# Eight layers in one kernel on one core: another list of spare products for TensorE

## The chip, the cores and the metric

The kernel runs as one program on one core of a Trainium2 chip. The metric is device time in microseconds (us). The engines are TensorE (PE, with its weight loads shown apart as PEld), VectorE (DVE), ScalarE (ACT), GpSimd (POOL) and SyncE (SP), which only issues DMAs. TensorE runs at one of two clocks, 1.2 or 2.4 GHz; the profile gives the granted one as a share, 0.5 or 1.0.

## The reference

A tensor x of 2048 tokens by 128 channels passes eight layers, each added to x and fed with a layer norm of it:

```
x = x + L0_attn_a(norm(x))   # delta rule: a recurrence over all 2048 tokens, 16 heads of 8x8 state
x = x + L0_ffn(norm(x))      # shared expert and 8 routed ones, top 2
x = x + L0_attn_b(norm(x))   # top 15 of causal logits, gather, small MLP, palette lookup
x = x + L0_ffn(norm(x))
x = x + L1_attn_a(norm(x))   # linear attention, running sums over tokens
x = x + L1_ffn(norm(x))      # sigmoid gate, 8 experts, top 2, relu squared
x = x + L1_attn_b(norm(x))   # decayed state, a recurrence over tokens
x = x + L1_ffn(norm(x))
```

The first one is what can't be spread over tokens:

```
v_old = einsum('bhd,bhde->bhe', k_t, state)
delta = clip(v_t - v_old, -1, 1)
state = state + clip(0.9 * k_t[..., :, None] * delta[..., None, :], -1, 1)
o = clip(einsum('bhij,bhj->bhi', state, q_t), -1, 1)
```

## The kernel before

The 2048 tokens are 16 tiles of 128. Each layer is one or more stages, each a Python generator over the tiles, written once for each engine (front, gram, scan and out for the first layer, pal and mix for the third, lin and dec for the two attentions of L1, ffn0 used twice a tile as ffn2 and ffn4, ffn1 used twice as ffn6 and ffn8, and prep once). A yield cuts a stage into pieces. Tiles of different layers are in work at the same time.

For each engine a long string, ORDER, gives the order of the pieces, one letter for each: z prep, f front, g gram, s scan, o out, a ffn2, p pal, m mix, b ffn4, l lin, c ffn6, d dec, e ffn8. PE's string has 2250 letters. fast() (line 501) walks it: for place n it calls before(n) and then runs the next piece of that letter. Each engine works its instructions strictly in this order; between engines there are only semaphores. The first layer's recurrence (stage scan) runs on DVE (L1033 multiplies, L1041 scans, 1024 steps), and PE gives it two sets of small products for every four steps: four of L610 (32x32, they need DVE's transpose L1013) and four of L621 (they need DVE's mask L1049; DVE reads them at L1056, later in its own order).

A float32 product counts as two in the profile, a bfloat16 product or a transpose as one.

Spare products are PE work whose result nobody reads: 128x128 weights of ones, 512 columns, bfloat16, line 541. How many stand at a place of the order is one digit of the string FILL (lines 200 to 221, 2250 digits). For PE before(n) is fill(n), and the digit is used in bank(), which hands a piece its PSUM bank:

```
533        def bank(key, *until):
535            b, old = bk.take(key, *until)
536            held.extend(old)
537            if idle[0]:
538                free()
539                w.wait_ge(*PV.at("b1", 0))
540            for _ in range(idle[0]):
541                e.matmul(b[:, 0:512], onesb[:, :], ..., start=True, stop=True)
542            idle[0] = 0
543            return b
550        def fill(n):
551            idle[0] = int(FILL[n])
```

So they are written into the bank that the piece then uses, after the wait for that bank and before the piece's other waits. Not every piece takes a bank. In scan the pieces with L610 write into psS, a tile of their own, and at both ends of the recurrence there are empty pieces; in mix the three loops with L764, L788 and L797 write into pb; prep's L950 does too; out's and lin's carry products (L643, L834) and the later pieces of the loops L708, L810 and L929 go on in a bank that an earlier piece took.

Other lines that the steps below name: norm() on PE (L564, a transpose; POOL's L1738 makes what it reads, ACT's L1369 reads its result), front's products (L573, L576; read by ACT L1378, and down that chain DVE L993), gram's (L596, read by ACT L1434), ffn1's up-products (L871, three groups of four; ACT reads each with L1658 and squares it with L1662) and down-products (L880 and L881, two groups, the first of which waits for the second square and the second for the third; read by ACT L1670).

Of the kernel before, what the change touches and what calls it, by code (L numbers as in the profile page):

```python
# [92 lines left out]
def pieces(stage):  # L93
# [104 lines left out]
        "ppppmpppmpppmppmpppmppppmppppmppmppppmpmpppppmpmpppmppepemeppppmpeepemeeeeeeeeee",  # L198
}
FILL = (  # L200
    "091909062040000000025030020020010000010010000100100000010000500001020020000070000901000001020000000000000020"
    "200002000200000000000000000010010001000000100500002000000000000000200000000000000000000000000000400000000001"
    "000000000010000000000110030000000000010000000000100000000020000000000000000000000000000520000000030000000300"
    "000000000000002000020000000010000000000000000000101000000000000000000000000000010000000000000200000000030000"
    "000000000000000002020000000000000200000000000300020000000000010000000000000000000001300000000000000000000000"
    "000000000000000000000000001003001010000000000100300000006000100000000000000000000000000000000000000000000000"
    "000000000000000020000000000000000000000000000100000000000002000000000000003220000000030103000000100300200000"
    "000000000000000000000000000000000000000000000002200000000000000000000000000000000000000000000010000000000010"
    "000000000000003000000000000000000000000000000000000000004030000000000000000000001000000000000000000000000000"
    "000000004000000000000000000000500000000000000000012000000000003000000000100000000000000000100000000000000000"  # L210
    "400000000000000000000000000000000000000000200000000000000000000000000020000520000000006030000000000002000000"
    "000000000000000000000000000000000000000000000000000000000000000000000400000000200000000000000330090006000000"
    "000000000000000000000000000000005000000000000000000000000000000000000000000000000000000000000000000003000000"
    "040000000000000020020003000213000080000000000000000000000000000000000000000000000000000000000000000010000000"
    "000000000002000000001000000000001040000000000001000000000000301000300000005000000000000000000000000100000000"
    "000000000000000000000000000000000000000000000000000000000000000100000000000000000041000000060000000000000050"
    "000000000100000010000000000000200000000000000200040000000000000000000000000000000000000000000000005000000000"
    "820930000000000000020100000000000000000000000000004000100000000000000000200000000000000000000400000000020000"
    "009300472001000000000000000000000000000000000000000000200000000000000000000000000000000000000000062540000100"
    "010000901000010200000000000000100000000000000000000000000000100000000000020000000300000000000000000000000000"  # L220
    "000000001200023000700160100000000001020000000000920005000000920930000200004200000920000920")

# [1951 lines left out]
```

## Time and profile before

| | us |
|---|---|
| median of 3 runs | 1384.04 |
| lowest and highest | 1383.59, 1386.72 |
| the profiled execution | 1393.87 |
| its span, first to last instruction | 1392.1 |
| PE, DVE, POOL, ACT busy in it | 1243.0, 1000.2, 910.7, 820.1 |
| mean granted clock | 0.929 |

The span is all of the profiled execution but 1.8 us; this execution was 9.8 us above the median, so a difference is worked out in its times and then added to the median. Busy time of PE is the union of its products' recorded times, and a recorded product ends some 0.17 us after its last column went in, so short waits of PE are not seen as idle time. In a row of a view an instruction stands with its line in the kernel, and the releaser in brackets is what ended the idle time before it.

### The profile page before, as it was taken

The page shows a single profiled execution, that of the slowest core. Times are in us where ns is not written, and L with a number is a line of the kernel's source. Part 1 is how long each engine was busy: PE and PEld are TensorE (multiplying, and loading weights), DVE is VectorE, ACT ScalarE, POOL GpSimd, SP SyncE. Part 2 cuts the span into 40 slices and gives each one's busy share as a digit, 9 for nine tenths or more (in the row PEclk, how much of TensorE's full clock was granted, in tenths as well). Part 3 has the DMA queues.
Part 4 walks back from the last instruction along what each step waited for, and adds up shares of the span by engine and source line. Part 5 has one row for each costly group of instructions (what it writes and reads, how often), then busy time and mean ns, then how long its engine had stood idle before and what let it go on. Part 6 is the DMA issues. An engine that isn't in the chain of part 4 may idle for free. (4 is left out here: it accounts for less than half of the span.)

```text
span 1392.1 us, 47171 instructions
## 1 busy us (share of the span) xinstructions
PE 1243.0 (89%) x18561; PEld 813.5 (58%) x18561; DVE 1000.2 (72%) x4437; ACT 820.1 (59%) x2193; POOL 910.7 (65%) x1321
## 2 busy tenths in 40 slices
PE   7777797989999998998899999999999999998896
PEld 3333454656566575756656665755666565757654
DVE  3768878778777868787786888978888775464432
ACT  2232253556676576757476666657574657667764
POOL 5353668686968677685776676776857466674541
PEclk8687678989999999999999999999999999999998
DMA  6000101001000000000010000100001010101000
GB/s 175 2 1 5 30 12 31 24 15 28 12 20 19 16 21 11 24 15 19 14 27 12 15 24 8 29 8 23 15 6 32 6 39 10 34 15 31 4 3 7
DMA packets 27257, 29.35 MB, mean 21 GB/s; under 512 B 12146, under 2 KB 22291, under 8 KB 27027
## 3 DMA queue, kind: packets, MB, share of 16 engines
q0 software_dynamic: 8336, 16.73, 4.9%
q1 hardware_dynamic: 18690, 9.51, 2.5%
q8 instruction: 149, 2.44, 0.8%
q14 instruction: 82, 0.66, 0.2%
HBM read 24.90 MB, written 2.29 MB: 20 GB/s over the span
## 5 line engine op out<-in xcount | busy, mean ns | idle before, releaser
L1873 POOL DMA_INDIRECT sb<-table,sb x240 | 241.8, 1007 | 81.5 <-issue 51.1
L1041 DVE TENSOR_TENSOR_SCAN ps<-ps,sb 128x47 f32<-128x47 f32 (+3 forms) x1024 | 271.0, 265 | 30.5 <-ACT sb L1445 1.5
L1033 DVE TENSOR_TENSOR ps<-sb,ps 128x24 f32<-128x24 f32 (+3 forms) x1024 | 193.1, 189 | 14.7
L541 PE MATMUL ps<-sb 128*128 128x512 bf16 x585 | 177.6, 413 | 8.7 <-ACT sb L1658 2.7
L1733 POOL TENSOR_TENSOR sb<-sb 128x1 f32<-128x1 f32 x128 | 73.2, 574 | 138.3 <-DVE sb L976 137.6
L610 PEld LDWEIGHTS ps<-sb 32*32 32x32 f32 x2032 | 41.0, 108 | 107.6 <-DVE sb L1013 65.6
L610 PE MATMUL ps<-sb 32*32 32x32 f32 x2032 | 69.8, 209 | 36.2 <-DVE sb L1013 35.6
L621 PEld LDWEIGHTS ps<-sb 32*32 32x32 f32 x2032 | 41.5, 108 | 93.1 <-DVE sb L1049 54.3
L982 DVE TENSOR_TENSOR sb<-ps,sb 128x128 f32<-128x128 f32 x112 | 32.2, 289 | 80.5 <-PE ps L708 29.8
L541 PEld LDWEIGHTS ps<-sb 128*128 128x128 bf16 x585 | 54.7, 105 | 58.8 <-issue 14.5
L1369 ACT ACTIVATE sb<-ps 128x128 f32<-128x128 f32 x128 | 34.9, 275 | 90.7 <-PE ps L564 90.2
L621 PE MATMUL ps<-sb 32*32 32x12 f32 x2032 | 64.7, 189 | 19.0 <-DVE sb L1049 10.0
L1056 DVE TENSOR_TENSOR ps<-sb,ps 128x12 f32<-128x12 f32 x254 | 40.9, 161 | 51.7 <-PE ps L621 50.3
L708 PE MATMUL ps<-sb 128*128 128x128 f32 x512 | 77.3, 298 | 0.0
L1670 ACT ACTIVATE sb<-ps,sb 128x128 bf16<-128x128 f32 x256 | 70.8, 375 | 8.2 <-PE ps L881 8.0
L596 PE MATMUL ps<-sb 128*128 128x480 f32 x128 | 73.8, 665 | 1.4 <-DVE ps L1056 0.5
L1049 DVE TENSOR_TENSOR sb<-ps,sb 128x32 f32<-128x32 f32 x254 | 45.9, 181 | 39.2 <-PE ps L610 38.1
L1885 POOL TENSOR_TENSOR sb<-sb 128x512 f32<-128x512 f32 (+1 forms) x32 | 47.3, 1485 | 36.0 <-DVE sb L1239 35.8
L764 PE MATMUL ps<-sb 128*16 128x16 f32 x4096 | 64.6, 211 | 6.3 <-issue 4.2
L708 PEld LDWEIGHTS ps<-sb 128*128 128x128 f32 x512 | 68.9, 209 | 1.9 <-issue 1.1
L1772 POOL TENSOR_TENSOR sb<-sb 128x480 f32<-128x480 f32 x64 | 66.0, 1034 | 4.9 <-ACT sb L1408 4.3
L764 PEld LDWEIGHTS ps<-sb 128*16 128x16 f32 x4096 | 54.3, 133 | 24.8 <-issue 18.4
(313 smaller groups left out, 3532.3 us busy)
## 6 DMA issues: line engine op xcount, KB each, us to landing
sb<-table,sb POOLq DMA_INDIRECT x240
sb<-in_cs SPq DMA_DIRECT2D x16, 128.0 KB
table<-sb SPq DMA_DIRECT2D x17, 64.0 KB, 1.5
sb<-dscr SPq DMA_DIRECT2D x64, 2.0 KB
out<-sb SPq DMA_DIRECT2D x16, 64.0 KB, 1.6
sb<-in_x SPq DMA_DIRECT2D x3, 256.0 KB, 5.4
sb<-in_wex SPq DMA_DIRECT2D x1, 512.0 KB, 4.1
sb<-in_rvx SPq DMA_DIRECT2D x1, 512.0 KB, 4.5
```

The costliest lines, as they stand in the source:

```text
L541: e.matmul(b[:, 0:512], onesb[:, :], onesb[:, :].unsqueeze(1).to_broadcast([128, 4, 128]), start=True, stop=True)
L596: e.matmul(b[:, 0:32 * LW], blk, g_.pp[j % 2][:, :], start=True, stop=True).then_inc(*g_.P("s"))
L610: x = e.matmul(psS[rows, 0:32], KZT[c % 2][rows, 32 * o1:32 * o1 + 32], R[g % 2][rows, :], start=g == 0, stop=True, skip_group_check=True)
L621: x = e.matmul(b[rows, 0:12], SB[g % 2][rows, :], KM[c2 % 2][rows, 4 * o2:4 * o2 + 4, :].rearrange("p a b -> p (a b)"), start=True, stop=True)
L708: x = e.matmul(b[:, 0:128], s.hw[j // 4][:, 128 * (j % 4):128 * (j % 4) + 128], wex[:, 128 * j:128 * j + 128], start=False, stop=j == 7)
L764: x = e.matmul(pb[32 * q:32 * q + 16, 16 * k:16 * k + 16], PTt[:, at, :], PTt[:, at, :], start=True, stop=True)
L1033: e.tensor_tensor(at(psP, p + ROW - 3 - 2 * m, [ROW, 3], [2, m], [1, 2]), AC[:, row(n, k), :, HIST - 2 * m:HIST].rearrange("p r (a b) -> p ...
L1041: e.tensor_tensor_scan(at(psD, 16 + k + COMB * skip, [COMB, 3 * ROW - skip]), at(psP, p + skip, [1, 3 * ROW - skip]), Q[:, i % 32, skip:3 ...
L1670: x = e.activation(s.w[:, 128 * at:128 * at + 128], bk.of[s.name, "d", g, c][:, 128 * j:128 * j + 128], ACT.Copy, scale=t[:, 40 + at:41 + at])
L1733: e.tensor_tensor(st[:, 11:12], st[:, 10:11], mhalf[:, 0:1], ALU.pow).then_inc(*s.G("lr"))
L1772: e.tensor_tensor(g_.pp[j % 2][:, :].rearrange("p (a b c) -> p a b c", b=2, c=LW), at(KT[c % 3], 32 * j, [2, 16], [0, 2], [1, LW]), km[:, ...
L1873: e.indirect_dma_start(GA[:, k, :], None, table[0:128 * i + 128, :] if i else table0, bass.IndirectOffsetOnAxis(u[:, k:k + 1], 0)).then_in ...
```

## The change

Only the string FILL differs. The order of the pieces, all stages and all other engines are the same. The old string has 204 digits that aren't zero, with the sum 585; the new one 506, with the sum 1619. Its first three lines of 21, and the last:

```diff
 FILL = (
-    "091909062040000000025030020020010000010010000100100000010000500001020020000070000901000001020000000000000020"
-    "200002000200000000000000000010010001000000100500002000000000000000200000000000000000000000000000400000000001"
-    "000000000010000000000110030000000000010000000000100000000020000000000000000000000000000520000000030000000300"
...
-    "000000001200023000700160100000000001020000000000920005000000920930000200004200000920000920")
+    "001949080000100100025330020120913090215310000000100000010020500001020002103075009901200000220020003000000020"
+    "200062010200000000000004210303010051400000000500502310930000000000200300000000000390000400000000400400002000"
+    "300260000100000020502110330002013000211000000003100803002020030000201000001050800200000520002200010030000000"
...
+    "000000000000002000010260000000100000000200013000922004000108010920000002000319014820009400")
```

## Rows read from the trace of the kernel before

**Rows 1.** The page: busy us of each engine, its share of the span, instructions.

```profile
PE 1243.0 (89%) x18561; PEld 813.5 (58%) x18561; DVE 1000.2 (72%) x4437; ACT 820.1 (59%) x2193; POOL 910.7 (65%) x1321
```

**Rows 2.** Windows: length, busy us of PE, PEld, DVE, ACT, POOL, granted clock, DMA.

```profile
0.00:300.00 300.00, 240.28 (x3067) 133.87 (x3068) 218.07 (x1132) 110.42 (x309) 178.98 (x308) 0.78 0.13 34
300.00:1140.00 840.00, 779.40 (x12459) 524.60 (x12458) 667.32 (x2985) 544.29 (x1447) 600.82 (x854) 0.97 0.07 18
1140.00:1392.10 252.10, 223.31 (x3038) 155.03 (x3036) 114.83 (x323) 165.36 (x438) 130.93 (x160) 0.98 0.06 15
```

**Rows 3.** The same windows for L541 alone; its durations in ns (min/median/max).

```profile
0.00:300.00 300.00, 53.21 (x146) 14.69 (x146) 0.78 0.13 34
300.00:1140.00 840.00, 77.63 (x264) 23.44 (x264) 0.97 0.07 18
1140.00:1392.10 252.10, 46.76 (x175) 16.54 (x175) 0.98 0.06 15
...
L541 PE MATMUL ps<-sb x585: 379/379/634, 1.1 to 1379.7; 128*128 128x512 bf16 x195
```

**Rows 4.** Instructions in order of time near the end: start, length in us.

```profile
1375.60 0.83 PE L871 MATMUL ps<-sb 128*128 128x128 bf16 x12
1376.27 2.11 PE L541 MATMUL ps<-sb 128*128 128x512 bf16 x9
1378.98 0.23 PE L880 MATMUL ps<-sb 128*128 128x128 bf16 x1 [0.60 <-ACT sb L1662]
...
1378.83 0.58 ACT L1658 ACTIVATE sb<-ps 128x512 bf16<-128x512 f32 x1
...
1379.98 0.35 ACT L1670 ACTIVATE sb<-ps,sb 128x128 bf16<-128x128 f32 x1
```

**Rows 5.** The chain of waits of the page, shares of the span by engine.

```profile
POOL 5%; PE 4%; issue 3%; ACT 1%; DVE 0%; DMA 0%; POOLq 0%; DVEq 0%
```

**Rows 6.** The page's group of L610: busy us, mean ns, idle before, releaser.

```profile
L610 PE MATMUL ps<-sb 32*32 32x32 f32 x2032 | 69.8, 209 | 36.2 <-DVE sb L1013 35.6
```

**Rows 7.** The scan's L621 near 592 us and its reader on DVE.

```profile
592.43 0.25 PE L621 MATMUL ps<-sb 32*32 32x12 f32 x8
...
596.40 0.17 DVE L1056 TENSOR_TENSOR ps<-sb,ps 128x12 f32<-128x12 f32 x1
```

**Rows 8.** The same near 1035 us: PE, DVE, ACT.

```profile
1035.28 0.25 PE L621 MATMUL ps<-sb 32*32 32x12 f32 x8
1035.46 1.07 PE L596 MATMUL ps<-sb 128*128 128x480 f32 x2
...
1037.66 0.27 PE L564 MATMUL ps<-sb 128*128 128x128 f32 x1
...
1037.95 0.15 DVE L1056 TENSOR_TENSOR ps<-sb,ps 128x12 f32<-128x12 f32 x1
...
1037.97 0.28 ACT L1369 ACTIVATE sb<-ps 128x128 f32<-128x128 f32 x1 [0.78 <-PE ps L564]
```

**Rows 9.** The start: PE's first products, and what two of them wait for.

```profile
1.12 4.02 PE L541 MATMUL ps<-sb 128*128 128x512 bf16 x9 [1.12 <-DVE sb L1315]
...
3.96 0.81 POOL L1738 TENSOR_SCALAR sb<-sb 128x128 f32<-128x128 f32 x1
...
6.66 0.88 PE L573 MATMUL ps<-sb 128*128 128x384 f32 x2 [0.88 <-DMA sb<-in_cst]
...
14.47 0.35 DVE L993 RECIPROCAL sb<-sb 128x32 f32<-128x32 f32 x1 [2.55 <-DMA sb<-in_bcm]
```

**Rows 10.** The scan's L1041 on DVE in four stretches at either clock.

```profile
142.40:166.30 23.90, 7.73 (x29) 0.50 0.13 35
183.40:200.50 17.10, 5.60 (x21) 1.00 0.04 10
200.50:220.90 20.40, 5.08 (x19) 0.50 0.10 25
220.90:268.70 47.80, 15.96 (x60) 1.00 0.10 25
```

More of the change, by code:

```diff
@@ L200 @@
 FILL = (
-    "091909062040000000025030020020010000010010000100100000010000500001020020000070000901000001020000000000000020"
-    "200002000200000000000000000010010001000000100500002000000000000000200000000000000000000000000000400000000001"
-    "000000000010000000000110030000000000010000000000100000000020000000000000000000000000000520000000030000000300"
-    "000000000000002000020000000010000000000000000000101000000000000000000000000000010000000000000200000000030000"
-    "000000000000000002020000000000000200000000000300020000000000010000000000000000000001300000000000000000000000"
@@ L206 @@
[L206 to L220, printed above, removed]
@@ L221 @@
-    "000000001200023000700160100000000001020000000000920005000000920930000200004200000920000920")
+    "001949080000100100025330020120913090215310000000100000010020500001020002103075009901200000220020003000000020"
+    "200062010200000000000004210303010051400000000500502310930000000000200300000000000390000400000000400400002000"
+    "300260000100000020502110330002013000211000000003100803002020030000201000001050800200000520002200010030000000"
+    "002000040070000000023003249310000003000300014002001000000003700000000400002020003300000000000100200032033000"
@@ new lines @@
+    "000000200000000002020000002001000000000002040309022000000100028003100000000000000001008000000000000000000000"
+    "000000000000000020000001103100535001100000010100330040006000000000000000000000000000000000500000000000005130"
+    "800000000000200020000000000000000000000300003100750000100002005022000000003220100000001201400000040330200030"
+    "200312430000000020050203900000000200100000001045000003000000000300000000000200000000000000000000000000000013"
+    "000000004000103000000000000000000300002079010000320010090000030000220000000000000000200000000000000000000000"
@@ new lines @@
+    "000000000000000000000000000000501001000000080009012000000000000000000000100000000000020602000000020000050000"
+    "400003004000440200010000000000000001000000300020000000000000000000000000000000000325021030310030020003000000"
+    "002400000000500010000000000020020023000020000220000900001000010000000604200600000000000000000400090006000020"
+    "500002000600040000001000000410302011406000000003000020000000000000000000046000002000000000000002000009000000"
+    "040100006000001023020020350003000061020000000000000000000000003000000003000000000000050000000000000020000040"
@@ new lines @@
+    "090000000000000000000000006910000000003100001000000580000000401000300000006534321550000000000000300000000000"
+    "001000000003000031000033000000300003000000001000004010100000000100001000140140000040200009000000000700100000"
+    "071001002000001000000002300210000030130010103000130000402003004000000000000003000000020200050000215300020700"
+    "005960000003500363000000000000000000000000000300003000000000100309080201000000090000000000000000000000000000"
+    "049000850000000000000004020240200003001000000330000200000000000000000020000000000000000000003600063004000000"
@@ L226, in program @@
+    "400200902000000000000042046204010200000004300000020006060000200022000000000003002405600000200010000201222000"
+    "000000000000002000010260000000100000000200013000922004000108010920000002000319014820009400")
 def program(nc, t):
```

## Prediction

> **What bounds the kernel now.** I read the table of engines first [rows 1]. TensorE (PE) is busy 1243.0 of 1392.1 us, DVE 1000.2, POOL 910.7, ACT 820.1. The reader is to see that PE, which runs every layer's pieces in one written order, has only 149.1 us of recorded idleness. Then three windows, for the clock [rows 2]: in the first 300 us the granted clock is 0.78, so PE spent (1 - 0.78) x 2 x 300 = 132 us at 1.2 GHz; from 300 to 1140 us it is 0.97 (some 50 us), after that 0.98 (some 10 us).
>
> Then the spare products themselves, line 541 [rows 3]. There are 585 of them, 146, 264 and 175 in the same three windows. Nine in a row take 2.11 us and the median one alone 0.38, so the next starts (2.11 - 0.38) / 8 = 0.216 us after the one before [rows 3, 4]: that is what one costs PE at 2.4 GHz, and about twice that at 1.2 GHz. All 585 are 126 us. In the trace they mostly stand directly ahead of a wait, as the nine of 1376.27, after which PE still waits 0.60 us for ACT L1662 [rows 4]: they lie in time in which PE had nothing to do, and cost nothing.
>
> Last, who holds the end. The chain of waits, which the profile can follow back only through the last 13% of the span, gives PE 4% and POOL 5% [rows 5]. So PE is about 4/13 = 0.3 of the path where the path is seen. PE itself waits longest ahead of the scan's products L610, 36.2 us, for DVE's transpose L1013 [rows 6].
>
> **What the change really executes.** The diff gives another string FILL and nothing else. fill(n) (line 550) puts the digit of place n into idle[0], overwriting what is there; only bank() (line 533) spends it. A place of the order whose piece doesn't call bank() drops its digit. I walked ORDER["PE"] through the stage functions: 1400 of the 2250 places call bank(). All 204 places of the old string are among them, and its sum, 585, is the count of L541 in the trace [rows 3]. Of the 506 places of the new one 299, with 1011 of the 1619 spare products, are among the 850 that don't call it: 130 in mix (its loops into pb), 100 in scan (the L610 pieces and the empty ones at both ends) and 69 elsewhere. So 608 products at 207 places are executed. Of the 585, 365 stay where they are; 220 go and 243 come, net +23.
>
> **Part 1, the net number.** 23 x 0.216 = +5.0 us of PE time, the upper end, if nothing hides it; the lower end is 0, PE having 149.1 us of idleness to put it in [rows 1]. I take +0.5: near 0, because almost all of the 585 stand in such idleness, as [rows 4] shows.
>
> **Part 2, the 220 that move.** The question is whether their new place is still free. Setting the trace's products against the order, 60 of some 95 places that lose products still have a wait behind them (144 products, 31 us): removing them only lengthens that wait. The others give back at most 76 x 0.216 = 16 us. Of the 243 that come (52 us), only some 7 us fall on a wait at the very same place. That looks bad, but the new place is mostly one or two pieces ahead of the old one, and what counts is when the piece behind is read. Four examples, two of them among the thirteen places that gain five or more (85 products in all), and the start:
> - Place 2246, near the end: 0 to 9 ahead of the third up-product group of the last FFN, and 9 to 4 at the next place, 2 to 0 after it. Its four L871 begin at 1376.05 (twelve from 1375.60, 0.056 each); with 1.94 us ahead, at 1377.99, done by 1378.4. ACT reads them at 1378.83 [rows 4]. The next group (L880, 1378.98) would start at 1378.22 + 4 x 0.216 = 1379.08, 0.1 us late, and ACT L1670 takes it at 1379.98. Cost 0.
> - Place 919: 0 to 9 ahead of L621 of 592.43, whose result DVE L1056 reads at 596.40 [rows 7]; with 1.94 us it is done by 594.7. The next two places lose 7. Cost 0.
> - Place 1709: 0 to 9 ahead of L621 of 1035.28, and 6 to 0 two places on. L1056 reads at 1037.95, in time. But the L596 of 1035.46 behind it moves to 1037.40 and would keep PE until 1038.3, while L564 ran at 1037.66 and ACT had already waited for it [rows 8]. Cost 0.6 us, if ACT L1369 is on the path.
> - Place 1, the first of all: 9 to 0. In the trace these nine run at 1.2 GHz from 1.12 to about 4.9 us, and L564 behind them could not start before POOL L1738 ended at 4.77 [rows 9]. Without them PE is idle at first, and the clock may rise later. Then the L573 and L576 from 6.66 to 8.2 us would take up to 1.3 us more; but DVE L993, two steps down that chain, waits for a DMA until 14.47 [rows 9]. Cost 0, at most 1.3.
> So a moved product costs between 0 and its 0.216 us, and most cost 0. Where none of it were hidden the thirteen big places alone would be 85 x 0.216 = 18 us; the lower bound is the gain of 16 us above, which I don't expect either, as what PE gains ahead of a wait it gives back in the wait. With a path share of 0.3 for the example's kind of miss, at a quarter of the thirteen, 13 x 0.25 x 0.6 x 0.3 = +0.6 us. Nothing is queued differently on DVE, ACT, POOL or SP: no wait and no DMA is changed.
>
> **Part 3, the clock.** Spare products only pay if they keep the clock at 2.4 GHz where it now falls. In the first 300 us the executed number goes from 146 to 127 (nine of the nineteen are place 1's), so I expect no gain there. Later single short stretches remain, 60 us in all by the windows. What one is worth: between 142 and 269 us the trace has two long stretches at 0.50 and two at 1.00 [rows 10]. The scan makes 29 + 19 = 48 steps in 44.3 us at 1.2 GHz (1.08 per us), 21 + 60 = 81 in 64.9 us at 2.4 GHz (1.25 per us). So a microsecond at 1.2 GHz loses 0.13 us of progress, the pace being set by DVE as much as by PE. If 10 us flip either way that is 1.3 us; taken 0.
>
> The Trainium skill prices this otherwise: TensorE: Matmul & The Clock Gate, in its table of terms, gives the penalty as throttled time x (1 - K/N), which at 1.2 GHz is 0.5 us for each microsecond. By that rule the 10 us would be 5 us and not 1.3, and the sum could be 1380 or 1390 in place of 1385. The scan's pace in this trace bears out only a quarter of it. The Trainium skill, TensorE: Matmul & The Clock Gate, Back-to-back issue gap, gives some 131 ns for a product of 512 columns in a sustained stream, by which the net 23 would be 3 us; nine in a row in this trace show 216 ns, and the measurement decides.
>
> **The sum.** Against the profiled execution: span 1392.1, total 1393.9 us, 9.8 us above the median 1384.0 of the runs shown; I take differences and add them to the median. 0.5 + 0.6 + 0 = +1, 1384.0 + 1 = 1385 us. What the measurement can tell from no change is about 0.2%, 2.8 us.
>
> **The rivals.**
> - A, no net change (above): 1385. For it: the executed count moves by 4%, 365 of 585 stay, and moved ones keep readers that come later [rows 4, 7].
> - B, slower: PE delays reach the path. The mechanism is place 1709's, spare products ahead of a piece whose reader follows at once. PE is in order and 89% busy, so a delay of 2 us is not made up for several pieces. If half of the 85 products at the thirteen big places pass through it is 9 us, 1393. It decides from 2.8 us on, which is 13 products, one in seven of the 85. For it: only 7 of 52 us fall on a wait at the same place; against it: 31 us of products vanish from in front of waits right behind.
> - C, faster: the added products lie where the clock fell. Were a third of the late 60 us to go back to 2.4 GHz, it is 20 x 0.13 = 2.6 us by the scan's pace and 10 at most if PE alone set it; with some of the 16 us of part 2 given back, 1384 - 6 = 1378. Against it: the first 300 us, where two thirds of the loss is, get fewer.
> - D, all 1619 are executed. 1034 x 0.216 = 223 us, more than the 149 us of idleness: even with all of it filled +74 us, 1458; if in return all of the 192 us at 1.2 GHz [rows 2] ran at twice the speed, 96 us less, 1362. The middle is 1410. The page would show L541 x1619. By the code this can't be.
>
> **How the numbers follow.** A 0.41, B 0.32, C 0.25, D and anything else 0.02. Faster by over 0.2% is C with half of the rest, 0.26; within 0.2% is A, 0.41; slower is B with the other half, 0.33. Predicted 1385, A's own range 1381 to 1388. The range of 8 in 10 reaches C's 1378 and B's 1393 with a little beyond, as the path before the last 13% isn't seen: 1376 to 1394.
>
> **What would show it.** L541 x608 in the page, some 127 of them before 300 us. PE busy up by about 5 us or less. The granted clock 0.92 to 0.94. Before DVE L1056 no new waits near 592 and 1035 us; under B the 0.78 us that ACT L1369 waits for L564 [rows 8] are over 1 us. PE's wait for ACT L1662 near the end [rows 4] is shorter than 0.3 us in any case. The prediction is wrong if L541 isn't 608, if the clock of the first 300 us leaves 0.78 by more than 0.05, or if the scan ends more than 3 us from where it did, which would say that delays of PE add up in it.

## The result: 0.9% slower, at the same clock

The changed kernel takes 1401.12 us (median of 9 runs, 1396.22 to 1405.42), the kernel before on the same chip 1386.72 (9 runs, 1383.17 to 1394.96): a ratio of 1.0092 with a 95% interval of 1.0072 to 1.0113. That is 13 us more by the ratio (the medians differ by 14), outside the range of 1376 to 1394. The page of the changed kernel, its busy times and its chain of waits by engine (of before: [rows 1, 5]):

```profile
PE 1230.2 (88%) x18584; PEld 814.4 (58%) x18584; DVE 1000.2 (72%) x4437; ACT 821.4 (59%) x2193; POOL 910.1 (65%) x1321
...
PE 40%; POOL 17%; issue 10%; DVE 9%; ACT 6%; DMA 0%; POOLq 0%; DVEq 0%; ACTq 0%
```

The windows of after (length, busy us of PE, PEld, DVE, ACT, POOL, granted clock, DMA), first of all instructions, then of L541 alone (of before: [rows 2, 3]):

```profile
0.00:300.00 300.00, 235.61 (x3070) 131.74 (x3071) 221.83 (x1147) 113.29 (x313) 181.39 (x311) 0.79 0.13 34
300.00:1140.00 840.00, 773.79 (x12471) 525.41 (x12469) 661.67 (x2960) 542.61 (x1442) 596.73 (x850) 0.98 0.07 18
1140.00:1394.40 254.40, 220.81 (x3053) 157.28 (x3049) 116.66 (x332) 165.47 (x439) 132.03 (x162) 0.99 0.06 15
...
0.00:300.00 300.00, 46.92 (x127) 12.85 (x127) 0.79 0.13 34
300.00:1140.00 840.00, 87.97 (x307) 27.39 (x307) 0.98 0.07 18
1140.00:1394.40 254.40, 45.47 (x174) 15.69 (x174) 0.99 0.06 15
```

The reader is to see three things. L541 stands 127 + 307 + 174 = 608 times, so the 299 digits at places without bank() are not executed. The clock isn't lower in any window. And the chain, here followed through 82% of the span, is 40% PE: half of what is seen, where I had taken 0.3 from the visible 13% of before. The chain of e4_tail, which has before's list up to place 1885, is followed through 81% and is 38% PE: so before's own share was nearer to a half too.

One caution on the pair of traces. The profiled execution of after took 1396.22 us, the shortest of its nine and with 0.938 the one of the highest clock (0.928 to 0.938); that of before 1393.9, near the longest of its own. So the two traces differ by 2.3 us only, not by the 13 to 14 us of the runs, and no stage can be read off by laying them side by side. Two kinds of difference lie in them: what the list does, and how long the clock happened to be low. The second can be taken out. Call 2 x (1 - granted clock) x time the "low time" (us at 1.2 GHz). Within the runs of the unchanged kernel before, on four chips (98 runs in five groups), the time rises by 0.29 to 0.34 us for each us of low time. I use 0.3. That range was seen within some 35 us of low time to either side of a mean; where a list moves it further, the last column rests on the price holding there too, which no run shows. The table does this for every kernel that ran, against the mean of before on the same chip (one of f_min's twelve runs, in a slower state, is left out):

| kernel | L541 | ratio [95%] | mean us | low time | left at 0.3 |
|---|---|---|---|---|---|
| e1_dropped | 608 | 1.0089 [1.0055, 1.0124] | +11.4 | -2.8 | +12.2 |
| e2_start | 566 | 1.0024 [0.9995, 1.0053] | +2.9 | +2.0 | +2.3 |
| e3_middle | 628 | 1.0054 [1.0028, 1.0080] | +7.8 | -2.5 | +8.6 |
| e4_tail | 584 | 1.0018 [0.9994, 1.0041] | +1.4 | -0.8 | +1.6 |
| g_tight | 779 | 1.0095 [1.0057, 1.0134] | +14.6 | -13.8 | +18.8 |
| g_slack | 778 | 1.0102 [1.0063, 1.0142] | +15.7 | -7.2 | +17.9 |
| f_min | 365 | 1.0077 [1.0044, 1.0111] | +13.1 | +47.8 | -1.2 |
| f_none | 0 | 1.0316 [1.0269, 1.0364] | +49.4 | +293.7 | -38.7 |
| k_local | 593 | 1.0019 [0.9990, 1.0047] | +3.2 | +3.0 | +2.3 |
| g_slack2 | 778 | 1.0077 [1.0054, 1.0101] | +10.9 | -7.6 | +13.2 |
| g_tight2 | 779 | 1.0155 [1.0124, 1.0186] | +22.9 | +14.6 | +18.5 |
| f_max | 828 | 1.0135 [1.0092, 1.0178] | +17.3 | -4.6 | +18.7 |
| s_swap | 608 | 1.0110 [1.0061, 1.0159] | +14.3 | +26.4 | +6.4 |
| f_min2 | 365 | 1.0147 [1.0104, 1.0189] | +19.9 | +64.3 | +0.6 |
| m_cut | 363 | 1.0109 [1.0068, 1.0150] | +14.6 | +93.9 | -13.6 |
| v_move | 582 | 1.0170 [1.0133, 1.0208] | +23.8 | +61.5 | +5.3 |
| v_late | 582 | 1.0146 [1.0116, 1.0176] | +19.5 | +55.1 | +3.0 |

The intervals reach 0.2 to 0.5% to either side, so a mean is good to 3 to 7 us. By the scatter of the runs the last column is good to 2 to 3 us at the price of 0.3 (4 us for f_none); with 0.34 in its place f_none's would be -50, m_cut's -17 and f_min2's -2. The four g_tight, g_slack, f_min and f_none of the first set ran on a slower chip, on which before took 1453.7 us at a clock of 0.909; each is compared with before on that chip.

### The profile page after: what moved, and what is told of

It reads as the page before. It is cut to its first block, busy times and chain, and to the rows that moved or that the text cites. A ratio compares the mean times of both kernels' runs of the same rounds, so it can differ in the third digit from the quotient of the medians.

```text
span 1394.4 us, 47224 instructions
## 1 busy us (share of the span) xinstructions
PE 1230.2 (88%) x18584; PEld 814.4 (58%) x18584; DVE 1000.2 (72%) x4437; ACT 821.4 (59%) x2193; POOL 910.1 (65%) x1321
## 4 chain that ended last, share of the span: by engine, by line
PE 40%; POOL 17%; issue 10%; DVE 9%; ACT 6%; DMA 0%; POOLq 0%; DVEq 0%; ACTq 0%
POOL sb L1873 5%; PE ps L764 3%; PE ps L708 3%; PE ps L541 3%; PE ps L831 2%; POOL sb L1733 2%; PE ps L834 2%; PE ps L621 2%; PE ps L736 2%; PE ps L596 2%; PE ps L610 1%; POOL sb L1885 1%; PE ps L640 1%; DVE ps L1041 1%; PE ps L788 1%
## 5 line engine op out<-in xcount | busy, mean ns | idle before, releaser
L1041 DVE TENSOR_TENSOR_SCAN ps<-ps,sb 128x47 f32<-128x47 f32 (+3 forms) x1024 | 270.9, 265 | 30.4 <-ACT sb L1445 1.5
L541 PE MATMUL ps<-sb 128*128 128x512 bf16 x608 | 180.4, 407 | 5.2 <-POOL sb L1822 2.5
L610 PEld LDWEIGHTS ps<-sb 32*32 32x32 f32 x2032 | 40.8, 108 | 106.1 <-DVE sb L1013 67.2
L610 PE MATMUL ps<-sb 32*32 32x32 f32 x2032 | 69.4, 208 | 36.0 <-DVE sb L1013 35.0
L621 PEld LDWEIGHTS ps<-sb 32*32 32x32 f32 x2032 | 41.1, 107 | 95.8 <-DVE sb L1049 58.4
L541 PEld LDWEIGHTS ps<-sb 128*128 128x128 bf16 x608 | 55.9, 104 | 56.9 <-issue 13.1
L621 PE MATMUL ps<-sb 32*32 32x12 f32 x2032 | 64.4, 188 | 24.1 <-DVE sb L1049 14.8
L1369 ACT ACTIVATE sb<-ps 128x128 f32<-128x128 f32 x128 | 35.1, 276 | 85.9 <-PE ps L564 85.2
L1056 DVE TENSOR_TENSOR ps<-sb,ps 128x12 f32<-128x12 f32 x254 | 40.7, 160 | 50.8 <-PE ps L621 49.3
L1670 ACT ACTIVATE sb<-ps,sb 128x128 bf16<-128x128 f32 x256 | 70.9, 377 | 5.4 <-PE ps L881 5.2
L764 PE MATMUL ps<-sb 128*16 128x16 f32 x4096 | 64.3, 211 | 5.9 <-issue 3.8
```

Of the source, the lines that this page charges most:

```text
L541: e.matmul(b[:, 0:512], onesb[:, :], onesb[:, :].unsqueeze(1).to_broadcast([128, 4, 128]), start=True, stop=True)
L610: x = e.matmul(psS[rows, 0:32], KZT[c % 2][rows, 32 * o1:32 * o1 + 32], R[g % 2][rows, :], start=g == 0, stop=True, skip_group_check=True)
L621: x = e.matmul(b[rows, 0:12], SB[g % 2][rows, :], KM[c2 % 2][rows, 4 * o2:4 * o2 + 4, :].rearrange("p a b -> p (a b)"), start=True, stop=True)
L764: x = e.matmul(pb[32 * q:32 * q + 16, 16 * k:16 * k + 16], PTt[:, at, :], PTt[:, at, :], start=True, stop=True)
L1041: e.tensor_tensor_scan(at(psD, 16 + k + COMB * skip, [COMB, 3 * ROW - skip]), at(psP, p + skip, [1, 3 * ROW - skip]), Q[:, i % 32, skip:3 ...
L1670: x = e.activation(s.w[:, 128 * at:128 * at + 128], bk.of[s.name, "d", g, c][:, 128 * j:128 * j + 128], ACT.Copy, scale=t[:, 40 + at:41 + at])
```

## The experiments

All of them change only the string FILL; each diff shows one line of it or the rule by which digits were chosen.

**Which part of the change?** First the dropped digits, then the new list in one of three stretches at a time. e1_dropped is the new list with

```
- digit of a place whose piece doesn't call bank(): as in the new list (1011 in all)
+ digit of a place whose piece doesn't call bank(): 0
```

> The new list with the digits of the 299 places that don't call bank() set to 0: sum 608 in place of 1619. The reading of the code says that these digits are never spent, so this must be the changed kernel again: L541 x608, and 13 to 15 us over the kernel before (1.009 to 1.010), as the change measured. If the dropped digits did something after all, it is near the kernel before or the count differs.

1403.49 us, +0.89%: the change's +0.92% again. The two theories of the count are settled, 608 products and not 1619 are what runs. The trace has it in one row (durations in ns, then first and last start):

```profile
L541 PE MATMUL ps<-sb x608: 376/379/634, 5.1 to 1388.1; 128*128 128x512 bf16 x152
```

The three stretches (e2_start: places 0 to 375, e3_middle: 376 to 1885, e4_tail: from 1886):

```
- FILL = old
+ FILL = old[:376] + new[376:1886] + old[1886:]     # e3_middle; the others in the same way
```

> New list up to place 375 (about the first 298 us), old list after: L541 x566. Theory 1 (spare products ahead of pieces whose readers follow at once delay the path): few are added here, so 0 to +2 us over the kernel before. Theory 2 (the start: 19 products fewer, nine of them the very first, keep the clock at 1.2 GHz longer or shift its stretches in the 300 us where it is low anyway): it carries nearly all of the loss, +10 to +14 us, and the granted clock of the first 300 us is under that of the kernel before.

> Old list up to place 375, new list for places 376 to 1885 (298 to 1140 us), old after: L541 x628, 43 more. Theory 1: most of the loss, +8 to +11 us. Theory 2: nothing, within 2 us. By the net number alone (43 x 0.216 us) +9 us at the most.

> Old list up to place 1885, new list after (from 1140 us on, behind the scan): L541 x584, one fewer. Theory 1: +2 to +4 us, since nothing behind it can take a delay back. Theory 2: within 1 us of the kernel before.

+0.24, +0.54 and +0.18%, together 0.96%. Only the middle is clear of nothing by its interval. There is no single culprit: the loss is spread, with most of it where most of the places are. It is not even, though: the middle adds 152 products and has 8.6 us left after the clock (0.26 us for each us of product), the tail adds 79 and has 1.6 (0.09), less than the 2 to 4 us that theory 1 expected there.

**Is it the number, the place or the clock?** f_min keeps the change's removals alone, f_none has no spare product at all, so part of the added work is left out; g_tight and g_slack add about the same number to the old list, in places that the trace of before tells apart.

```
- old digit
+ min(old, new)                                     # f_min: the 220 removed, none added
+ 0                                                 # f_none
+ old + added, where the next piece's reader already waits for it (73 places)   # g_tight
+ old + as many, where PE's wait holds them and no reader is late (93 places)   # g_slack
```

> Removals alone: at each place the smaller of the two digits, 365 products at 123 places, the 220 that the change takes away and none that it adds. Theory 1: not slower than the kernel before by more than 2 us, maybe 1 to 4 us faster, as some of the 220 stood ahead of prompt readers too. Theory 4: slower by most of the change's 13 us, with a lower granted clock.

> No spare product at all. It tells what the 585 are worth. Theory 1 says nothing of it but that the delays are gone: if the clock were worth little (0.13 us for each microsecond at 1.2 GHz by the scan's pace before) and the clock fell to 0.75 it is +30 us; by half a microsecond for each it is +100 us or more.

> The old list, nothing removed, plus 194 of the 243 products that the change adds: those at the 73 places where, in the trace of the kernel before, the 0.216 us of each product run out the slack of a reader of this piece or a next one (a reader on another engine starts less than that after the product it waits for, and no wait of PE lies between); L541 x779. Worked out place by place the readers would be late by 33 us in all. Theory 1 (prompt readers): at least as slow as the changed kernel, +12 to +25 us. Theory 3 (PE's total load counts, wherever it stands): 194 x 0.216 = 42 us, some 10 to 20 us of it on the path, and the same in the next run. Theory 4 (the cover that was taken away counts, as PE then idles and the clock falls): no change or faster.

> The old list, nothing removed, plus 193 products at 93 other places near the former ones (the same numbers in each third of the kernel), chosen so that no reader in the trace of the kernel before is reached: 16 us of their 42 us fall on waits of PE, the rest ahead of pieces read later; L541 x778. Theory 1: 0 to +4 us. Theory 3: as slow as the last run. Theory 4: no change or faster, with a higher granted clock.

f_none is the clearest: without the 585 products the clock falls to 0.814, low time grows by 294 us, and the kernel loses 3.2%. What is left after the clock is -38.7 us, or 0.31 us given back for each of the 126 us of products: by this working the 585 weren't free either, though 294 us is far outside the low time over which the price was seen. f_min loses 0.77%, and the price of its lower clock, 0.3 x 48 = 14 us, is all of its +13.1: the 220 removed products gave nothing back. g_tight and g_slack both lose 1%, and cannot be told apart. But their places came from a trace of a chip on which before takes 1384 to 1394 us, and they ran on one where it takes 1453.7. So the pair was run again on a chip of the faster kind, with before itself and a local probe.

> The list of before and 193 products more at 93 places which by the first trace of before have waits long enough to hold them with no reader delayed (778 executed); the same kernel as g_slack, on a chip whose trace has the timeline from which the places were picked. Theory 'place': where the products stand decides, so this one is within 0.4% of before while g_tight2 is 1% or more slower. Rival 'number': each us of added products costs some 0.4 us wherever it stands: 1.0 to 1.3% slower, as g_tight2.

> The list of before and 194 products more, at 73 places whose next product has a reader that by the first trace of before was waiting for it (779 executed); the same kernel as g_tight. Theory 'place': 1.2 to 2.5% slower than before and at least 0.8% slower than g_slack2. Rival 'number': 1.0 to 1.3% slower, no more than 0.3% from g_slack2.

Here the place does tell: +0.77% in waits, +1.55% ahead of prompt readers, with intervals that don't touch. After the clock it is 13.2 against 18.5 us, for 42 us of added products: 0.32 and 0.44 us for each us put in. Without any correction they are 12.0 us apart. Neither theory had it whole. Theory "place" said within 0.4% for g_slack2, and that failed: products that by the trace fit into waits still cost a third of their length. Rival "number" said at most 0.3% between the two, and they are 0.8% apart. On the slower chip the same two lists were 0.07% apart: there the place told nothing.

**One place looked at closely.** k_before is the unchanged kernel; k_local adds two of the change's groups.

```
- place 630: 0    place 912: 0
+ place 630: 5    place 912: 3
```

> The kernel before, unchanged, for a second trace of it on this chip. Both theories expect 1380 to 1395 us with its profile on a chip like the one that took the first traces, L541 x585, and PE's L584 of the place near 596 us some 8.2 us after the L573-type product that opens that stretch, as in the first trace of before.

> The list of before with two of the change's groups alone: 5 products at place 630 (ahead of L680) and 3 at place 912 (ahead of L810); 593 executed. Theory 'phase': products ahead of a prompt reader push the chain by less than their own time at once, and a small delay grows where it makes an instruction of VectorE overlap one of GpSimd: about +0.65 us from place 649 on, and about +1.9 us in the weight product L669 of place 922, with DVE L1152 near 596 us at 2.7 us in place of 0.9 us. The two groups alone then give about +2.5 us (0.2%). Rival 'load': only the products' own 1.7 us counts, at some 0.45 us per us: +0.8 us, and L1152 keeps 0.9 us.

k_before is one execution, of 1394.04 us; the median of before on this chip is 1388.96 (23 runs), that of k_local 1391.88. Instructions in order of time (start, length in us; in brackets the idle time before and its releaser), first of k_before, where POOL's L1795 starts after DVE's L1152 has ended:

```profile
594.68 0.65 PE L810 MATMUL ps<-sb 32*32 32x128 f32 x16
594.91 0.17 DVE L1056 TENSOR_TENSOR ps<-sb,ps 128x12 f32<-128x12 f32 x1 [0.23 <-PE ps L621]
...
596.37 0.37 ACT L1456 ACTIVATE sb<-ps,sb 128x128 f32<-128x128 f32 x1 [0.67 <-PE ps L633]
...
597.25 0.43 DVE L1147 SCALAR_TENSOR_TENSOR sb<-sb 128x256 f32<-128x256 f32 x1 [0.61 <-ACT sb L1493]
...
597.96 0.88 DVE L1152 SCALAR_TENSOR_TENSOR sb<-sb 128x256 f32<-128x256 f32 x1
...
598.46 0.85 POOL L1760 TENSOR_TENSOR sb<-sb 128x256 f32<-128x256 f32 x1
...
599.28 2.09 POOL L1795 TENSOR_TENSOR sb<-sb 128x512 f32<-128x512 f32 x2
...
600.29 1.11 DVE L1130 TENSOR_TENSOR sb<-sb 128x8 f32<-128x8 f32 x1
...
601.65 0.23 PE L669 MATMUL ps<-sb 128*24 128x128 bf16 x1 [0.77 <-DVE sb L1132]
```

and the same stretch of k_local:

```profile
587.25 0.82 PE L541 MATMUL ps<-sb 128*128 128x512 bf16 x3
587.38 0.18 DVE L1056 TENSOR_TENSOR ps<-sb,ps 128x12 f32<-128x12 f32 x1 [0.23 <-PE ps L621]
...
588.00 0.67 PE L810 MATMUL ps<-sb 32*32 32x128 f32 x16
...
589.49 0.37 ACT L1456 ACTIVATE sb<-ps,sb 128x128 f32<-128x128 f32 x1 [1.32 <-PE ps L633]
...
590.38 0.72 DVE L1147 SCALAR_TENSOR_TENSOR sb<-sb 128x256 f32<-128x256 f32 x1 [1.26 <-ACT sb L1493]
...
591.38 2.73 DVE L1152 SCALAR_TENSOR_TENSOR sb<-sb 128x256 f32<-128x256 f32 x1
591.75 2.09 POOL L1795 TENSOR_TENSOR sb<-sb 128x512 f32<-128x512 f32 x2
...
595.58 0.17 DVE L1130 TENSOR_TENSOR sb<-sb 128x8 f32<-128x8 f32 x1
...
596.00 0.23 PE L669 MATMUL ps<-sb 128*24 128x128 bf16 x1 [2.14 <-DVE sb L1132]
```

Up to L1056 k_local runs 594.91 - 587.38 = 7.53 us ahead (its low stretches fell elsewhere). The three products put L810 back by 7.53 - 6.68 = 0.85 us. ACT's L1456 waits 1.32 in place of 0.67: the 0.65 us of three products reach it whole. POOL doesn't move along: its L1795 is still 599.28 - 591.75 = 7.53 us ahead. So DVE's work has slipped against POOL's by 0.65 us, and that changes what falls together. L1147 takes 0.72 us in place of 0.43, which leaves L1152 6.58 us ahead (597.96 - 591.38). L1152 then meets L1760 and both L1795 and takes 2.73 us in place of 0.88; in k_before the second L1795 falls on L1130 instead, which takes 1.11 us there and 0.17 in k_local. The net of these two is 1.85 - 0.94 = 0.91 us, and L669 behind them is only 5.65 us ahead: 1.88 us lost from 0.65 us of products. That is what was forecast for the place (about +1.9), and the same 2.73 us stands in after, e1_dropped and e3_middle, all with the new digits there.

Over the whole kernel, though, such overlaps largely cancel. All 32 of L1152 together are 22.1 us in these three and 20.1 to 20.5 in before, e2_start and e4_tail; L1130 has 10.5 in after against 12.0 in before; and DVE's busy time as a whole is 1000.2 us in both, 1001.6 in e1_dropped, and 997.4 us in k_local against 997.8 in k_before. So most of the 12 us are not a DVE that is held up longer in the sum. The whole kernel, +0.19% [-0.10, +0.47], fits both the phase theory's 0.2% and the rival's 0.06%; the verdict is the place's, not the total's, and whether the 1.88 us last to the end isn't shown. The share at place 630 can't be read cleanly, since a low stretch of k_local falls beside it.

**Additions, removals and moves.** The last six ask whether the additions alone are the loss, and whether a list can be made better by the rule "not ahead of a prompt reader".

```
+ max(old, new)                                     # f_max: the 243 added, none removed
+ min(old, new) + g_slack2's 193 + 50 of the removed at their old places        # s_swap: 608
+ min(old, new)                                     # f_min2: as f_min, other chip
+ old without 222 products at 78 places with no wait of PE behind them          # m_cut: 363
+ m_cut + 219 at 99 places nearby whose wait holds them                         # v_move: 582
+ v_move from place 376 on (but for three single products), old before it       # v_late: 582
```

> The list of before with the change's 243 additions and none of its 220 removals (828 executed). Theory 'additions': their gross cost is the change's whole loss, +12 to +15 us, and the clock gives back 0.27 us for each us at 1.2 GHz that disappears (some 20 to 30 us of it, 5 to 8 us): +5 to +10 us (0.4 to 0.7%), with less than the change's 0.9%. Rival 'removals': the loss is in the removed products; then this kernel is within 0.2% of before or faster.

> 608 executed products as in the change: the 365 that it keeps, 193 at the slack places of g_slack2, and 50 of the removed ones back in their waits. Theory 'place': as the additions stand in waits, at 0.31 us per us (g_slack2) for 42 us, +13 us less what a higher clock gives, and removals cost nothing: +7 to +11 us (0.5 to 0.8%), under the change's 0.9%. Rival 'number alone': +12 to +15 us (0.9 to 1.1%). Rival 'the list of before is a selected point': as the change or worse, +12 us and more, with the clock as in before.

> Only the removals (365 executed), the same kernel as f_min on the slower chip, here beside m_cut. If the products that the change removes stood in waits: the clock's price alone, some 50 us more at 1.2 GHz x 0.27 = +13 us (0.95%), nothing given back.

> The list of before without the 222 products at 78 places that have no wait of TensorE behind them by the trace of before (363 executed, as many as f_min2 but for two). Theory 'place': each stood in the path's way, so removing 48 us of them gives back some 0.45 x 48 = 21 us against 13 us for the clock: -8 us, 0.6% faster than before, and 1.5% faster than f_min2. Rival 'number': as f_min2, some 0.9% slower than before.

f_max: +18.7 us after the clock for 52 us of products, 0.36 per us. The additions alone cost at least as much as the whole change, at an unchanged clock and before any correction (+17.3 us). So the rival "removals", which had this kernel within 0.2% of before, is out, though the total of +1.35% is above what either expected. f_min2: +0.6 after the clock, so the removals again give nothing back; their +19.9 us are above the 13 expected, as the clock fell by more. Each half of the change alone is thus slower than the two together: the removals alone lose 13 to 20 us through the clock, which in the change the added products hold up (low time -2.8 us in e1_dropped), and these cost it 12 us of delay in return. m_cut, with as many products taken from busy places, has 14 us less left than f_min2; but only 5.3 us of it is in the measured times, the rest is the price of 30 us more low time. It wasn't faster than before, as theory "place" had said, but 1.1% slower: its clock lost twice what I had put in. s_swap is as slow as the change (+1.10%, interval 0.61 to 1.59), now with 26 us more low time. Its total is what rival "number alone" said (0.9 to 1.1%), and theory "place" (0.5 to 0.8%) missed it; but a clock like that of before, which both it and the rival "selected point" took for granted, it hasn't, and only 6.4 us are left after it, 0.15 us for each us of product added. The windows of two of them (columns as above), to be read for the clock:

```profile
0.00:300.00 300.00, 234.61 (x3027) 132.28 (x3027) 218.58 (x1128) 110.06 (x308) 178.31 (x307) 0.77 0.13 34
300.00:1140.00 840.00, 756.93 (x12227) 516.29 (x12227) 658.30 (x2953) 543.79 (x1445) 593.95 (x846) 0.95 0.07 18
1140.00:1400.00 260.00, 223.12 (x3089) 162.13 (x3089) 124.30 (x357) 166.16 (x441) 138.05 (x170) 0.96 0.06 16
```

That is f_min2: 0.77, 0.95 and 0.96, where before has 0.78, 0.97 and 0.98 [rows 2]. And m_cut, lower in each:

```profile
0.00:300.00 300.00, 228.75 (x3009) 131.15 (x3010) 222.49 (x1145) 112.27 (x312) 180.82 (x310) 0.75 0.13 34
300.00:1140.00 840.00, 767.90 (x12300) 525.80 (x12298) 659.25 (x2953) 543.23 (x1442) 595.55 (x849) 0.94 0.07 18
1140.00:1400.00 260.00, 228.20 (x3031) 162.28 (x3031) 117.48 (x342) 165.74 (x440) 133.29 (x164) 0.94 0.06 15
```

The attempt to do better than before:

> 582 executed products, 3 fewer than before: the 222 at the 78 places with no wait behind them are taken away and 219 of them put at 99 places nearby whose wait in the trace of before holds them. Theory 'place': 13 us given back (m_cut against f_min2), 42 us put in at the slack price of 0.15 to 0.32 us per us, 6 to 13 us, at an unchanged clock: 0 to -7 us, the middle -3 us (0.2% faster). Rival 'selected list': any list that differs from before's in a third of its products is slower by 0.7% or more, as all six so far.

> As v_move from place 376 on alone (144 products taken away behind about 297 us, 141 put back nearby; the first 297 us as in before). Theory 'place': two thirds of v_move's gain, -5 to 0 us, with the clock of the first 300 us as in before. Rival 'selected list': slower by 0.4% or more.

In both theory "place" fell: +1.70% and +1.46%. Both are what the rival "selected list" forecast (0.7% and 0.4% or more); it says that the list of before is hard to better and gives no reason why. Windows of v_move:

```profile
0.00:300.00 300.00, 241.34 (x3059) 134.04 (x3059) 217.56 (x1129) 110.07 (x308) 178.02 (x306) 0.77 0.13 34
300.00:1140.00 840.00, 775.08 (x12229) 520.53 (x12228) 652.18 (x2934) 538.87 (x1426) 589.60 (x841) 0.95 0.07 17
1140.00:1410.00 270.00, 242.24 (x3276) 171.53 (x3275) 130.16 (x377) 172.00 (x460) 143.19 (x176) 0.97 0.07 18
```

At practically the same number (582 against 585) the clock is down from 0.97 to 0.95 in the middle, over the runs 61 us more low time, which is 18 of the 23.8 us. So where a spare product stands sets the clock too, and the products that looked like mere delay were among those that held it up, as m_cut shows, which only takes these away and has 94 us more low time. No list beat before's; every one that differed from it along the whole order was slower by 0.77% or more.

## Why the prediction was wrong, step by step

- **Right: what is executed.** 608 of L541, 127 of them before 300 us; the clock 0.938, between 0.92 and 0.94; the first 300 us at 0.79; the scan's last L1041 at 1142.3 in place of 1140.4 us. PE's busy time fell by 12.8 us where I had it up by at most 5, which fits its lower low time (2 x 0.062 x 1394 = 173 us against 2 x 0.071 x 1392 = 198): this execution had the highest clock of its nine.
- **Right: the removals** give nothing back: f_min and f_min2 leave -1.2 and +0.6 us after the clock. That PE gives back in the next wait what it gains is the forecast's reason, and fits.
- **Right: places 919, 2246 and 1709.** At 919 the nine products come, and L1056 reads with no wait. The rows of after near 1035 and near the end (of before: [rows 8, 4]):

```profile
1037.30 2.12 PE L541 MATMUL ps<-sb 128*128 128x512 bf16 x9
1039.35 0.25 PE L621 MATMUL ps<-sb 32*32 32x12 f32 x8
...
1040.22 0.15 DVE L1056 TENSOR_TENSOR ps<-sb,ps 128x12 f32<-128x12 f32 x1
1040.74 0.28 ACT L1369 ACTIVATE sb<-ps 128x128 f32<-128x128 f32 x1 [1.37 <-PE ps L564]
...
1378.65 2.11 PE L541 MATMUL ps<-sb 128*128 128x512 bf16 x9
1380.59 0.39 PE L871 MATMUL ps<-sb 128*128 128x128 bf16 x4
1381.68 0.22 PE L880 MATMUL ps<-sb 128*128 128x128 bf16 x1
...
1382.58 2.16 ACT L1670 ACTIVATE sb<-ps,sb 128x128 bf16<-128x128 f32 x8
```

  L1369 waits 1.37 us in place of 0.78, the 0.6 us worked out; that it is over 1 us was the sign named for rival B. Near the end all stands 2.60 us later than in before, L880 2.70: the 0.1 us worked out, and L1670, 2.60 later, doesn't feel it.
- **Wrong: part 2, "most cost 0", +0.6 us.** This is the step that failed. Measured, the 243 additions cost 18.7 us alone (f_max) and 12.2 us with the removals (e1_dropped): 0.36 and 0.23 us per us of product, where the sum had 0.6 for 52 us. I had four examples, mostly from big groups, and multiplied the miss of one by a share; the groups of one to four products, 158 of the 243, had no price at all. Place 912's three are of that kind, and cost 1.9 us by L669, almost three times their length. And I asked only whether the next reader was late, one step deep; g_slack2, chosen so that no reader is late, still loses 13 us.
- **Wrong: part 1's reason, that almost all of the 585 stand in idleness.** It rested on one group of nine. By the trace of before 222 of them, at 78 places, have no wait of PE behind them; m_cut, without these, has 13.6 us less left after the clock, and f_none, without any, 38.7. The +0.5 for the net 23 can't be told apart from the rest here: e4_tail, with one product fewer, and e2_start, with nineteen fewer, aren't faster.
- **Wrong: the path's share, 0.3.** After's chain gives PE 40 of 82, about half, and e4_tail's 38 of 81. It came from the last 13% of the span, the wrong stretch to speak for 1140 us of scan.
- **Wrong in size, without consequence for this change: part 3.** A us at 1.2 GHz costs 0.3 us, not the scan's 0.13. The Trainium skill's TensorE: Matmul & The Clock Gate, in its table of terms, would have it 0.5; the runs of before show 0.29 to 0.34, between the two. Since the clock of the change stayed (low time -2.8 us), this moved nothing.
- **The rivals.** B was right in mechanism and in sign, and too small: 9 us against 12 to 13. It counted half of the big groups at full price and nothing for the small ones. C failed on its own point, as almost no low time went away. D couldn't be and wasn't: the same kernel with the 1011 digits struck out is as slow.

**What stays open.** Shown are the cost of the additions, that it isn't the clock, its spread over the stretches, and one place's chain over some 7 us. Not shown is the rest of the path from 243 products to 12 us: the place at 912 accounts for 1.9 of them. That delays grow on the whole through instructions of DVE and POOL that come to overlap is not borne out: L1152 and L1147 sum to 41.6 us in after and 37.9 in before, but L1130 goes from 12.0 to 10.5, and DVE is busy for 1000.2 us in both. Nor is it shown why v_move's clock fell, why products in apparent waits cost anything, or why the tail's additions cost so little.

## What to carry to other kernels

Price filler work on a nearly full in-order engine by a measured rate (here 0.3 to 0.44 of its length where it was only added, 0.3 even in apparent waits; 0.1 to 0.26 where other products went for it), and treat a cost of 0 as something to be shown for each place; readers one step away don't show it. A list of such fillers is bought for the clock, so compare kernels by two numbers, low time times its price and what is left, before naming a cause. And check first whether the profiled execution is typical of its kernel's runs: here the pair of traces showed 2 us of a loss of 13.

## What the runs showed of the hardware

- DVE's L1152 on 128x256 took 0.43 us as the median of its 32 in k_before (0.38 at the least), 0.88 us at 597.96 with parts of POOL's L1780, L1784 and L1760 beside it, and 2.73 us in k_local with L1760 and two L1795 on 128x512 beside it. L1130, on 128x8 only, took 0.17 us, and 1.11 us beside an L1795. The two L1795 took 2.09 us in either case. All of these work on SBUF only.
- Between runs of one kernel, one us more at 1.2 GHz went with 0.29 to 0.34 us more time, on all four chips, with TensorE busy for 89% of the span.
- Without its 585 spare products (126 us of TensorE's time) the kernel, on the slower chip, had a clock of 0.814 in place of 0.909 and took 3.2% longer.
- At the end of nine L541 (128*128) the L621 (32*32) starts 0.11 us later than the pace of 0.216 us gives (1039.35 against 1037.30 + 9 x 0.216 = 1039.24), and k_local's L810 (32*32; 588.00 against 587.25 + 3 x 0.216 = 587.90) 0.10. In the trace of before no L621 starts less than 0.309 us after an L541 (34 of them), while many 128*128 products start 0.216 us after one. So a spare group costs somewhat more than its products beside small tiles.
- The kernel before had medians of 1389 to 1392 us on three chips and 1453.7 on a fourth, where the two lists of added products could no longer be told apart.
